# First weight chunks on a second load queue, and the first rounding work redistributed, in a token-shift MoE kernel

## What is computed

```python
xprev = concatenate([shift_state[:, None, :], x[:, :-1]], axis=1)   # x: 8 x 1024 x 512
xk = x + (xprev - x) * time_maa_k
xr = x + (xprev - x) * time_maa_r
e_idx = token_ids * 5099 % 16                 # expert of a token; at most C = 512 tokens each
expert_in = ...                               # 16 x 512 x 512, gathered rows of xk
h = square(relu(einsum('ecd,edf->ecf', expert_in, w_key)))          # 512 -> 1024
expert_out = einsum('ecf,efd->ecd', h, w_value)                     # 1024 -> 512
r = sigmoid(einsum('btd,ed->bte', xr, w_recept))                    # 8192 x 512 times 512 x 512
out = x + r * y                               # y: expert_out put back in the tokens' order
```

## Time and profile before

| | |
|---|---|
| median of 3 runs | 886.61 us (886.07 to 887.07) |
| profiled execution | 886.43 us |
| its span, first to last instruction | 884.7 us |
| TensorE busy | 878.2 us, 99% of the span |
| granted TensorE clock | 1.000 of full speed over the span |

### The profile page before, as it was taken

How to read it: one execution, slowest core, us unless ns; L and a number is a source line. 1 busy time by engine, 2 the same in 40 slices (tenths; PEclk the granted TensorE clock), 3 DMA queues, 4 the chain that set the end, 5 groups by cost and what they waited for, 6 DMA issues and landing times.

```text
span 884.7 us, 10918 instructions
## 1 busy us (share of the span) xinstructions
PE 878.2 (99%) x3963; PEld 726.6 (82%) x3963; DVE 653.4 (74%) x894; ACT 499.4 (56%) x773; POOL 502.1 (57%) x471
## 2 busy tenths in 40 slices
PE   8999999999999999999999999999999999999998
PEld 7888888888888888888888888888888888888887
DVE  6987746859687777777787878787877777777742
ACT  7766656565556464646464737373737282828270
POOL 2000034465676777676767676767676767674142
PEclk9999999999999999999999999999999999999999
DMA  6675568675757575757575757575757565756341
GB/s 240 223 264 194 194 213 281 228 256 164 252 181 252 189 251 186 253 183 251 184 249 180 250 184 244 185 249 185 244 185 243 194 241 190 243 188 223 119 143 47
DMA packets 72533, 186.40 MB, mean 211 GB/s; under 512 B 10400, under 2 KB 10656, under 8 KB 72480
## 3 DMA queue, kind: packets, MB, share of 16 engines
q1 hardware_dynamic: 44672, 101.79, 34.1%
q0 software_dynamic: 27664, 83.91, 28.1%
q10 hardware_dynamic: 144, 0.00, 0.0%
HBM read 152.11 MB, written 33.55 MB: 210 GB/s over the span
## 4 chain that ended last, share of the span: by engine, by line
PE 98%; DMA 0%; issue 0%; DVE 0%; ACT 0%; SPq 0%; POOLq 0%; POOL 0%
PE acc L914 29%; PE acc L916 29%; PE acc L915 29%; PE rt_bank L916 3%; PE rt_bank L914 3%; PE rt_bank L915 3%; PE acc L926 1%; DMA xT<-xs_t 0%; PE rt_bank L994 0%; POOLq L99 0%; POOL out L446 0%; DVE mix L769 0%; ACT mix L502 0%; ACT xr_hi L510 0%; DVE gate L837 0%
## 5 line engine op out<-in xcount | busy, mean ns | idle before, releaser
L431 POOL DMA_INDIRECT pair_even<-pairs,row_pair x128 | 144.6, 1130 | 174.9 <-DVE row_pair L743 105.3
L543 ACT ACTIVATE hid<-acc 128x512 f32<-128x512 f32 x112 | 67.1, 600 | 208.3 <-PE acc L916 208.2
L431 POOL DMA_INDIRECT pair_odd<-pairs,row_pair x128 | 144.9, 1132 | 58.3 <-issue 32.9
L915 PE MATMUL acc<-wv_lo,h_hi 128*128 128x512 f32 (+1 forms) x456 | 176.6, 387 | 0.0
L916 PE MATMUL acc<-wv_hi,h_lo 128*128 128x512 f32 (+1 forms) x456 | 176.6, 387 | 0.0
L914 PE MATMUL acc<-wv_hi,h_hi 128*128 128x512 f32 (+1 forms) x456 | 176.6, 387 | 0.0
L914 PE MATMUL acc<-xk_hi,wk_hi 128*128 128x512 f32 x448 | 174.6, 390 | 0.0
L916 PE MATMUL acc<-xk_hi,wk_lo 128*128 128x512 f32 x448 | 174.5, 390 | 0.0
L915 PE MATMUL acc<-xk_lo,wk_hi 128*128 128x512 f32 x448 | 174.3, 389 | 0.0
L780 DVE TENSOR_TENSOR wv_lo<-raw,wv_hi 128x1024 fp32r<-128x1024 f32 x64 | 78.4, 1226 | 59.5 <-ACT wv_hi L531 59.5
L808 DVE TENSOR_TENSOR h_lo<-hid,h_hi 128x512 fp32r<-128x512 f32 x128 | 88.4, 691 | 35.2 <-ACT h_hi L552 35.2
(11 more groups left out here) (148 smaller groups left out, 1507.3 us busy)
## 6 DMA issues: line engine op xcount, KB each, us to landing
raw<-w_key SPq DMA_DIRECT2D x64, 512.0 KB, 5.5
raw<-w_value SPq DMA_DIRECT2D x64, 512.0 KB, 3.8
xT<-xs_t SPq DMA_DIRECT2D x13, 1026.0 KB, 7.6
gates<-gate SPq DMA_DIRECT2D x8, 1024.0 KB, 5.5
gates<-wr_raw SPq DMA_DIRECT2D x8, 1024.0 KB, 5.3
xT<-xs_t SPq DMA_DIRECT2D x11, 256.5 KB, 5.4
pair_even<-pairs,row_pair POOLq DMA_INDIRECT x128, 3.1
pair_odd<-pairs,row_pair POOLq DMA_INDIRECT x128, 2.9
```

Of the source, the lines that this page charges most:

```text
L431: pool.indirect_dma_start(pair[e % 2][:, i, :], None, pairs, bass.IndirectOffsetOnAxis(row_pair[:, a:a + 1], 0)).then_inc(s_pair[e % 2], 16)
L543: act.activation(hid[:, n % H_SLOTS, :], up_bank(*divmod(n, KF))[:, :], ACT.Relu).then_inc(s_relu, 1)
L915: pe.matmul(bank, hi, m_lo, start=False, stop=False)
```

## The change

Five things are done:

- The load of weight chunk 0 leaves SP's queue and goes to ACT's, ahead of `maar`. The load of chunk 1 goes there too, behind `maar`. SP goes straight from the token halves to the token chunks.
- For the left half of chunk 0, DVE computes the fused multiply-add twice: once with the rounded `xr_hi` as its output, once into `mix`. POOL's rounding copy of that half is gone.
- POOL rounds the right half of weight chunk 0, which DVE did before.
- DVE does the right half of `mix` (`mix_xr(0)`) ahead of `wr_lo` of chunk 0.
- PE does right hi x hi ahead of left `wr_lo`.

```diff
@@ SyncE
             sp.dma_start(xT[:, 0, 0, 0:1 + HALF], xs_t[0:P, 0:1 + HALF]).then_inc(s_x_left, 16)
-            load_w_recept(0)
-            load_group(0, 0)
-            for k in range(1, KD):
+            for k in range(KD):
                 load_group(0, k)
-                load_w_recept(k)
+                if k > 1:
+                    load_w_recept(k)
@@ GpSimd
-            pool.wait_ge(s_mix_left, 1)
-            pool.tensor_copy(xr_hi[:, 0, 0, 0:HALF], mix[:, 0, 0:HALF]).then_inc(s_hi_left, 1)
+            pool.wait_ge(s_wrec[0], 16)
+            pool.tensor_copy(wr_hi[:, 0, D // 2:D], wr_raw[:, 0, D // 2:D]).then_inc(s_wrhi_first, 1)
@@ ScalarE
+            act.dma_start(wr_raw[:, 0, :], w_recept_t[0:P, :]).then_inc(s_wrec[0], 16)
             act.dma_start(maar[:, :], maa_r[:, :]).then_inc(s_maar, 16)
+            act.dma_start(wr_raw[:, 1, :], w_recept_t[P:2 * P, :]).then_inc(s_wrec[1], 16)
             act.wait_ge(s_zeros, 1)
@@ VectorE, mix_left, split_left and the start
+                dve.scalar_tensor_tensor(xr_hi[:, 0, 0, 0:HALF], slot, factor, here,
+                                         ALU.mult, ALU.add).then_inc(s_hi_left, 1)
                 dve.scalar_tensor_tensor(slot, slot, factor, here, ALU.mult, ALU.add).then_inc(s_mix_left, 1)
             def split_left():
                 dve.wait_ge(s_hi_left, 1)
+                dve.wait_ge(s_mix_left, 1)
...
             mix_left()
-            dve.wait_ge(s_wrec[0], 16)
-            dve.tensor_copy(wr_hi[:, 0, D // 2:D], wr_raw[:, 0, D // 2:D]).then_inc(s_wrhi_first, 1)
             split_left()
+            mix_xr(0)
             dve.wait_ge(s_wrhi_first, 1)
             split_w_recept(0)
-            mix_xr(0)
             mix_xr(1)
@@ TensorE, receptance_left
                 first_pass(0, left, xr_lo, wr_hi)
+                pe.wait_ge(s_hi_right, 1)
+                first_pass(0, right, xr_hi, wr_hi, True)
                 pe.wait_ge(s_wrlo, 1)
                 first_pass(0, left, xr_hi, wr_lo)
-                pe.wait_ge(s_hi_right, 1)
-                first_pass(0, right, xr_hi, wr_hi, True)
                 first_pass(0, right, xr_hi, wr_lo)
```

## The result

The changed kernel takes 888.59 us (median of 10 runs, 887.79 to 889.57), the kernel before 886.70 in the same comparison. The ratio is 1.0022, with a 95% interval of 1.0013 to 1.0031. Forecast were 886.0 and 885.1 to 887.2. Its profiled execution took 888.54 us, with a span of 886.8.

A forecast was written before the change was run, and what follows sets the result against it. The prediction took TensorE's start as the bound: after it, one unbroken row of matmuls. Chunk 1 starting at 8.25 instead of 8.85 us saves 0.60: 886.43 becomes 885.83, plus 0.18 to the median gives 886.0 us, range 885.1 to 887.2.

The forecast's parts named there:

- T: Time at which VectorE starts the first multiply-add: 3.40 us before, forecast 4.0, bounds 3.6 and 5.6.
- The left half lands between 2.94 and 3.6; `maar` ... at 3.9: Start loads: 256 KB of weights now share the engines; 262 KB at 385 GB/s are 0.68 us.
- `maar` late: Rival: `maar` behind the weights holds up every matmul of chunk 0; at its bound 887.6 us; chance 0.16.
- T + 4.20: End of chunk 0's matmuls on TensorE, counted from T; 8.20 us with T = 4.0.
- T + 2.25: Start of right hi x hi on TensorE, after VectorE's multiply-add and GpSimd's copy (0.07 and 0.40).
- The rival's threshold of T = 4.65: First multiply-add later than 8.85 - 4.20 = 4.65 us makes the kernel slower, by the rival `maar` late.
- There is no clock to win: TensorE's clock is 1.00 from 6 to 9 us and from 14.42 to 200 us; no gain there.
- a loss of 1.8 needs T = 6.4: Losing 1.8 us takes a first multiply-add at 6.4 us; only something outside the rows does it, slower 0.04.
- the wait of 0.9 us: Sign: this wait of TensorE disappears and chunk 1 starts at 8.2 to 8.4 us, with no wait after it.
- the tokens of chunk 1 don't bind: Chunk 1's token load doesn't hold TensorE while it lands by 5.87 us; bounds 5.3 and 6.03.

The follow-up runs named there:

- warm_45: The changed kernel with 45 warm-up matmuls instead of 28: 887.25 us, ratio to the kernel before 1.0004.
- work_only: The changed kernel with all loads issued as in the kernel before: 886.57 us, ratio to the kernel before 0.9999.
- no_pool: warm_45 with GpSimd out of chunk 0, its work there given to ScalarE and VectorE: 886.89 us, ratio to the kernel before 0.9999.
- before_filled: The kernel before with 31 warm-up matmuls instead of 28 and 7 more between chunks 0 and 1: 886.69 us, ratio 0.9996.
- before_gap: The kernel before with 12 warm-up matmuls instead of 28: 887.53 us, ratio to the kernel before 1.0006.

## Why the prediction was wrong

Two steps failed. T was mis-sized, and the chain behind it was priced at durations and a clock that the change did not leave alone. The second did more. The forecast put chunk 1 at 8.25, and it started at 11.09, 2.8 us later: 1.05 from T, 0.61 from the chain, 1.23 from the pace of TensorE (the forecast had put 0.05 on top of its chain, which makes up the rest).

**T.** "The left half lands between 2.94 and 3.6; `maar` ... at 3.9" took 262 KB at 385 GB/s as the whole price of sharing. The left half was used at 4.10, and `maar` landed at 4.95. The mechanism (`maar` behind the weights, the left half beside them) was right; the term was 0.6 us and measured 1.65 (3.40 to 5.05). The chance was on the wrong side of it: 0.16 for `maar` late. The rate of 385 stands in a row at 3.00, and the row at 1.75 already had 58: the start of a stream was priced with the rate of its middle. By the prediction's own sum, though, T = 5.05 alone gives 9.25 for chunk 1, 0.40 behind the kernel before, or 887.0. That is inside the range.

**The chain behind T.** T + 4.20 was built of durations that VectorE and GpSimd have when they seldom work at once, as before. The change made them work at once. The link that slipped is right hi x hi, which waits for GpSimd's copy: T + 2.25 in the prediction, T + 2.86 in the changed kernel (7.91) and in warm_45 (7.86). The whole chain measured T + 4.81 in warm_45 and T + 4.30 without GpSimd. The rival's threshold of T = 4.65 came from the same T + 4.20, so it was too high as well.

**The clock.** "There is no clock to win" was read from two stretches with fast matmuls, and the prediction then took the fast pace as given for every matmul of chunk 0, without a reason. From 7.91 to the start of chunk 1 the same eight matmuls took 3.18 us in the changed kernel and 1.95 in warm_45, 1.23 less. This was in no rival. With T at 5.05 the prediction's own bound, "a loss of 1.8 needs T = 6.4", was passed all the same: 1.9 us were lost. In the changed kernel the pace also makes the time scatter, over 1.8 us against 0.3 in warm_45.

**What held.** The gain is bounded by the start; the wait of 0.9 us is gone; the tokens of chunk 1 don't bind (ScalarE's term of them is done at 6.69, and VectorE gets to it at 7.52); the new order of work costs nothing while the loads come as before (work_only); nothing opens behind 12 us (877.4 to 877.8 in every kernel). The difference of 0.22% is just over the 0.2% that the prediction took for the least that can be told from none.

**The sum as measured.** Changed kernel to warm_45, 888.50 - 886.87 less 887.25 - 886.87: 1.25 us of pace. warm_45 to no_pool: 0.60 of overlap. What is left, -0.22 us, can't be told from none. So in the medians the late T itself, without slow matmuls and without the overlap, costs nothing that shows. Yet no_pool starts chunk 1 at 9.45 in its trace, 0.60 behind the kernel before's 8.85. The profiled execution of before was one of its fastest (886.43, median 886.87), and by 877.5 its median run starts chunk 1 near 9.4. That its slower runs are runs with the left half near 3.5 is likely by the two traces above, but not shown for the timed runs; a slow first pair of matmuls, as in before_filled, is a rival that no run here sets apart. A version that beats both kernels did not come out: work_only, before_filled and no_pool are within 0.1% of the kernel before.

## What to carry to other kernels

A second queue is no second path: before moving a load to it, list what is in flight at that moment, and ask which urgent load now shares; a 2 KB constant behind 256 KB, and a token load beside it, made this kernel's first multiply-add 1.65 us later. A stall ahead of TensorE can cost twice, once as the stall and once as slow matmuls behind it (1.2 us here), so price it with both, and fill it with warm-up matmuls if it can't be removed. And work moved to an engine that idled beside VectorE brings its old duration only if it still runs while VectorE rests.

## What the runs showed of the hardware

- The start of two large loads issued together is poor: 41 to 78 GB/s from 2.0 to 2.5 us in seven traces, against 200 to 244 in the seven in which nothing large was issued beside the left half until 0.44 us later. From 3.0 us on the former reach 377 to 398 GB/s.
- The granted clock reads 1.00 from 6 to 7 us in before_gap while 512-wide matmuls start 0.43 us apart, twice the 0.23 of later ones. At the start of these traces the pace of the matmuls says at which level TensorE runs, and that column doesn't.
- TensorE is slow at first and becomes fast at a moment that differs between runs: 45 warm-up matmuls took 4.98 us in one trace and 4.52 in another.
- A 256-column copy on GpSimd takes 0.40 us at its fastest, and 0.47 to 1.46 us beside VectorE operations with two inputs, which lengthen in turn from 0.48 to 0.62 and from 0.68 to 1.22.
